# Two PSUM buffers for the scans' input in the state-space stage of a hybrid block

## The chip, the cores and the metric

The kernel is one program on one core of a Trainium2 chip. The metric is its time on the device in microseconds (us), the median of several executions; the profile comes from one more execution.

## The reference, cut to what matters

16 sequences of 256 positions and 128 features go through four residual blocks: a state-space block, a two-layer attention and feed-forward stack, a gated attention, and the same stack again. The change lies in the first, with these lines of it (width 256, 16 states):

```python
x = resid * lax.rsqrt(jnp.mean(resid * resid, -1, keepdims=True) + EPS) * norm_w
skip = x @ skip_w.T
xe = x @ in_w.T                       # then a causal convolution of 4 taps along time
xs = jax.nn.silu(xc)
delta = jax.nn.softplus(xs @ wd1.T @ wd2.T + wd2_b)
A = -jnp.exp(A_log); Bm = xs @ wb.T; Cm = xs @ wc.T
h = jnp.exp(d_l[:, :, None] * A) * h + (d_l * x_l)[:, :, None] * b_l[:, None, :]
y_l = jnp.einsum('ben,bn->be', h, c_l)
y = (y + xs * W_D) * jax.nn.silu(skip)
return resid + y @ out_w.T
```

## The kernel before, in words

**Stages.** The program runs a state-space stage ("m"), an attention and feed-forward stage ("f", 32 steps of one sequence and layer), the gated attention ("p") and "f" again. A layer norm ("n": st, mv, z on VectorE, ve, rs on GpSimd) stands in front of each.

**Tiling.** The state-space stage takes one sequence after another. Channels lie on the partitions, 256 as two halves (c), time along the free dimension. The 16 states are taken in eight groups g of two, so a tile of one group has 2 x 2 x 256 = 1024 columns. For each group:

- TensorE: bB(g) and bC(g) spread B's and C's rows over all partitions (two bf16 matmuls each, L526);
- ScalarE: a(g), four exponentials into m_a (L608), c(g), a copy of C's rows (L613);
- VectorE: bx(g), the product of delta x and B, written to PSUM (L639), and h(g), the scan over time, which reads it (L646);
- GpSimd: hc(g), the product of the states and C, as two instructions (L679);
- TensorE: y(g), the sum over states by the identity, into bank 1 (L533). y7 adds xs W_D.

Around it, once for a sequence: sq, me, rr, xr (the norm), xT and xTe (transpose and its copy), xe (convolution and projection in 16 passes, L498), xs, skip, gate, u and bc (L513), ue, hi, r1, mid, mid2, lo (B and C split in three bf16 parts), z, abs, exp, ln, delta, dx, and at the end yg, out, xx and x. xs and gate use another set of ScalarE's functions than the exponentials, so that two table loads come in each window.

**Order.** Each engine works through a list written out by hand. M_ORDER is the list of one window, in which each engine does every step once; M_STAGES says for each step how many windows it lags (0, 1 or 2), so for which sequence it is done there. The steady windows are 4 to 16. Before them stands START, a list with the first layer norms and windows 1 to 3, behind them MF with windows 17 and 18 and the first three of "f". An engine takes its list strictly in order; a step waits for semaphores of the steps that it names, and `m_before(..., g, back)` means group g - back, of this sequence or the one before.

**PSUM.** Eight banks of 512 columns: bank 0 and 1, pair 0, 1 and 2 (two banks each). In "m" before the change:

| place | holds |
|---|---|
| bank 0 | xT, u, bc |
| bank 1 | y, out |
| pair 0, first half | xe, skip, z (m_x_ps) |
| pair 0, second half | bC |
| pair 1, halves | bB, alternating by g |
| pair 2 | bx, the scans' input |

Of the kernel before, what the change touches and what calls it, by code (L numbers as in the profile page):

```python
# [64 lines left out]
class Stages:  # L65
# [13 lines left out]
    def done(self, step):  # L79
# [43 lines left out]
M_ORDER = {  # L123
    "dve": "bx1 h1 bx2 yg h2 bx3 h3 ue bx4 x h4 bx5 h5 r1 bx6 delta h6 lo bx7 h7 bx0 h0",
    "pe": "bB7 bB0 y4 bB1 bC0 y5 y6 bC1 y7 bB2 xT bC2 bB3 xe bC3 skip bB4 u bB5 out bc bC4 z bC5 y0 bB6 y1 bC6 y2 y3 "
        "bC7",
    "act": "xTe sq c2 a3 xs c3 gate a4 c4 a5 abs c5 exp hi ln a6 mid2 a7 c6 mid a0 c7 a1 c0 xr a2 c1",
    "pool": "dx hc6 xx hc7 me rr hc0 hc1 hc2 hc3 hc4 hc5"}
# [4 lines left out]
       for ph, stages in (("m", M_STAGES), ("f", F_STAGES), ("p", P_STAGES))}  # L133
# [21 lines left out]

MF = {
# [117 lines left out]
def build(nc, ins, out):  # L274
    with ExitStack() as ctx:
# [180 lines left out]
        def half(t, k):  # L456
            return t[:, 512 * k:512 * k + 512]

        m_x_ps = half(pair[0], 0).rearrange("p (c l) -> p c l", c=EC)
        m_xT_ps = bank[0][:, 0:L]  # L460
        m_u_ps = bank[0][0:DD, 0:L]
        m_bc_ps = bank[0][64:96, L:2 * L]
# [4 lines left out]
        def m_bcast(g, k):  # L467
            return (half(pair[0], 1) if k else half(pair[1], g % 2)).rearrange("p (n l) -> p n l", n=GN)
# [1113 lines left out]
```

## Time and profile before

| | |
|---|---|
| median of 3 runs | 2874.21 us (2873.69 to 2874.41) |
| the profiled execution | 2875.4 us, span 2873.6 us |
| mean granted TensorE clock | 0.977 of full speed |
| busy TensorE / VectorE / ScalarE / GpSimd | 2647.1 / 2260.1 / 2225.5 / 1223.4 us |
| the state-space stage | from the start to about 575 us |

Busy is the time in which an engine has an instruction at work. In a timeline the start is that of the instruction, and the next instruction can start a little before the one in front ends, since they overlap. "[1.16 <-ACT f_sq L872]" means that the engine was idle for 1.16 us before and that ScalarE's write of f_sq at line 872 released it. PE is TensorE, DVE VectorE, ACT ScalarE, POOL GpSimd.

### The profile page before, as it was taken

Reading aid. Unit: us, or ns where it says so; the run is one execution under the profiler, and the core shown is the slowest. Engines: PE = TensorE matmul, PEld = TensorE weight load, DVE = VectorE, ACT = ScalarE, POOL = GpSimd, SP = SyncE. Lnnn points to the kernel's source line nnn. Section 1 sums busy time; section 2 is a strip of 40 time slices with the busy share of each in tenths; the row PEclk is TensorE's granted clock in tenths of the full one; section 3 lists DMA queues with packets and bytes.
Section 4 is the critical chain, followed back from the end, with each engine's and each line's share of the span. In section 5 each row is a group of like instructions: output and inputs, shape, how many; then the busy total and the mean of one; then the engine's idle time right before and its main releaser. Section 6 shows DMA issues by size and latency. Waiting matters only on the chain. (4 is left out here: it accounts for less than half of the span.)

```text
span 2873.6 us, 55943 instructions
## 1 busy us (share of the span) xinstructions
PE 2647.1 (92%) x18868; PEld 1819.6 (63%) x18868; DVE 2260.1 (79%) x3798; ACT 2225.5 (77%) x6114; POOL 1223.4 (43%) x1089
## 2 busy tenths in 40 slices
PE   6888888789999999999999999997899999999997
PEld 3454445356666666666777777774566666666665
DVE  8999999976767777777689999996667777676774
ACT  5788878557777777777799999995677777777775
POOL 5776777664444444444400000001444444444442
PEclk8999999999999999999999999997999999999998
DMA  3000000000000000000000000000000000000000
GB/s 98 1 1 1 1 1 1 0 1 2 1 1 1 13 13 1 1 1 1 13 14 2 2 2 1 2 1 1 1 2 1 1 2 13 17 5 7 7 7 7
DMA packets 15672, 17.84 MB, mean 6 GB/s; under 512 B 3838, under 2 KB 12863, under 8 KB 15295
## 3 DMA queue, kind: packets, MB, share of 16 engines
q1 hardware_dynamic: 15390, 14.26, 1.7%
q8 instruction: 156, 2.56, 0.4%
q14 instruction: 126, 1.02, 0.1%
HBM read 12.16 MB, written 2.10 MB: 5 GB/s over the span
## 5 line engine op out<-in xcount | busy, mean ns | idle before, releaser
L1064 POOL TENSOR_TENSOR f_p<-f_p,f_rs 128x512 f32<-128x512 f32 (+1 forms) x256 | 321.2, 1255 | 907.4 <-DVE f_rs L1013 907.3
L901 ACT ACTIVATE f_p<-pair,f_nm 128x128 f32<-128x128 f32 (+1 forms) x1024 | 387.4, 392 | 125.2 <-DVE f_nm L1002 125.2
L679 POOL TENSOR_TENSOR m_hc<-m_h,m_c 128x512 f32<-128x512 f32 x256 | 323.4, 1284 | 154.5 <-DVE m_h L646 120.5
L1056 POOL TENSOR_TENSOR f_qb<-f_kn,f_tab 128x512 f32<-128x512 f32 x256 | 373.5, 1480 | 24.3 <-DVE f_kn L981 21.0
L646 DVE TENSOR_TENSOR_SCAN m_h<-m_a,pair 128x1024 f32<-128x1024 f32 x128 | 292.2, 2283 | 11.6 <-ACT m_a L608 1.9
L767 PE MATMUL pair<-f_wqkv,f_hT 128*128 128x512 f32 x512 | 248.7, 609 | 18.0 <-DVE f_kn L981 14.5
L608 ACT ACTIVATE m_a<-m_delta,m_A 128x255 f32<-128x255 f32 x512 | 217.3, 496 | 59.4 <-DVE m_h L646 58.8
L533 PE MATMUL bank<-m_hc,ident 128*128 128x512 f32 x512 | 248.2, 619 | 1.4 <-DVE X L655 1.3
L815 PE MATMUL pair<-ident,f_p 128*128 128x128 f32 x1536 | 244.7, 282 | 3.7 <-DVE f_pT L1007 2.4
L855 PE MATMUL bank<-f_hnT,f_w 128*128 128x256 f32 (+1 forms) x768 | 213.4, 401 | 12.5 <-ACT f_g L933 3.1
L815 PEld LDWEIGHTS pair<-ident,f_p 128*128 128x128 f32 x1536 | 170.6, 141 | 82.2 <-issue 60.0
L1002 DVE TENSOR_REDUCE f_nm<-pair 128x4 f32<-128x512 f32 (+1 forms) x256 | 208.3, 814 | 16.0 <-PE pair L802 13.6
L802 PE MATMUL pair<-f_kT,f_qT 64*128 64x128 f32 (+1 forms) x2048 | 211.1, 325 | 0.0
L901 ACT ACTIVATION_READ_ACCUMULATOR f_p<-pair,f_nm 128x1 f32 x1024 | 209.5, 205 | 0.0
L829 PEld LDWEIGHTS pair<-f_pT,f_v 128*64 128x64 f32 x3072 | 150.5, 137 | 91.5 <-issue 91.1
L971 DVE TENSOR_REDUCE f_ss<-f_sq 128x16 f32<-128x1024 f32 x128 | 155.5, 1215 | 64.3 <-ACT f_sq L872 64.3
L829 PE MATMUL pair<-f_pT,f_v 128*64 128x128 f32 (+1 forms) x3072 | 199.0, 265 | 2.0 <-DVE f_pT L1007 2.0
L1150 PE MATMUL pair<-p_kT,p_qT 128*128 128x256 f32 (+1 forms) x1024 | 193.1, 331 | 3.0 <-ACT p_a L1226 1.7
L1234 ACT ACTIVATE p_p<-p_s,p_rm 128x256 f32<-128x256 f32 (+1 forms) x512 | 192.0, 464 | 3.6 <-DVE p_rm L1302 3.2
L802 PEld LDWEIGHTS pair<-f_kT,f_qT 64*128 64x128 f32 x2048 | 148.5, 188 | 68.7 <-issue 68.7
L784 PE MATMUL bank<-ident,f_qa 128*128 128x128 f32 x1024 | 165.0, 284 | 14.3 <-DVE f_qa L995 8.0
L1219 ACT ACTIVATE p_e<-pair,p_hgT 128x256 f32<-128x256 f32 (+1 forms) x512 | 173.2, 429 | 4.8 <-PE bank L838 2.1
(181 smaller groups left out, 6159.2 us busy)
## 6 DMA issues: line engine op xcount, KB each, us to landing
f_wqkv<-in_f_wqkv SPq DMA_DIRECT2D x4, 768.0 KB, 4.0
out_x<-X SPq DMA_DIRECT2D x16, 128.0 KB, 1.8
f_w<-in_f_w SPq DMA_DIRECT2D x4, 341.0 KB, 3.3
f_wo<-in_f_wo SPq DMA_DIRECT2D x4, 256.0 KB, 2.7
sel<-in_sel SPq DMA_DIRECT2D x1, 768.0 KB
f_w<-in_f_w SPq DMA_DIRECT2D x4, 192.0 KB, 3.2
m_taps<-in_m_taps SPq DMA_DIRECT2D x1, 512.0 KB, 3.6
X<-in_x SPq DMA_DIRECT2D x1, 512.0 KB, 8.5
```

What stands on the lines that cost most here:

```text
L533: mm = nc.tensor.matmul(bank[1][:], ident[:], m_hc[:, g % 4, n].rearrange("p c l -> p (c l)"), start=g == 0 and n == 0, stop=False, skip_g ...
L608: op = nc.scalar.activation(m_a[:, g % 2, n, c, 1:L], m_delta[:, b, c, 1:L], ACT.Exp, scale=m_A[:, c, g * GN + n:g * GN + n + 1])
L646: op = nc.vector.tensor_tensor_scan(m_h[:, g % 2].rearrange(flat), m_a[:, g % 2].rearrange(flat), pair[2][:], 0.0, ALU.mult, ALU.add)
L679: op = nc.gpsimd.tensor_tensor(m_hc[:, g % 4, n], m_h[:, g % 2, n], m_c[:, g % 2, n].unsqueeze(1).broadcast_to([P, EC, L]), ALU.mult)
L767: mm = nc.tensor.matmul(half(pair[0], x), f_hT[:, t * P:t * P + P], fw["wqkv"][:, x * 512:x * 512 + 512], start=True, stop=True)
L802: mm = nc.tensor.matmul(SC[:, slot(h), k0:k1], f_qT[r, b, h // 2, t * P:t * P + P], f_kT[r, b, h // 2, k0:k1], start=False, stop=True, ski ...
L815: mm = nc.tensor.transpose(PT_PS[:, j * P:j * P + P], f_p[:, t, j, y * P:y * P + P], ident[:])
L829: mm = nc.tensor.matmul(OT_F[DH * e:DH * e + DH, c, q0:q1], f_v[:, b, y, h, :], w, start=y == 1 or t == 0, stop=y == 0, skip_group_check=True)
L855: mm = nc.tensor.matmul(bank[1][0:HR[c], e * L:e * L + L], fw["w1"][:, x * HID + c * P:x * HID + c * P + HR[c]], f_hnT[:], start=True, sto ...
L901: op = nc.scalar.activation(f_p[:, t, j, k0:k1], SC[:, j, k0:k1], ACT.Exp, bias=f_nm[:, t, j:j + 1], accum_out=f_sm[:, t, j:j + 1])
L1056: op = nc.gpsimd.tensor_tensor(f_qb[:, t, :, o].rearrange("p (x h) d -> p x h d", x=2), f_kn[:, t, :, 32 - 32 * e:64 - 32 * e].rearrange(" ...
L1064: op = nc.gpsimd.tensor_tensor(f_p[:, t, :, k0:k1], f_p[:, t, :, k0:k1], f_rs[:, t, :].unsqueeze(2).broadcast_to([P, 4, k1 - k0]), ALU.mult)
```

## The change

The scans' input gets two buffers, pair 1 and pair 2 by turns. For that B's broadcast gets one bank (pair 0, first half) where it had two, C's keeps one, and xe, skip and z move into bank 0 to xT, u and bc. The waits follow: bx(g) waits for h(g-2) where it waited for h(g-1); bB(g) for bx(g-1) where it was bx(g-2); xT for delta of the sequence before where it was lo; u and bc for gate where it was xs; z for r1 besides ue; the first qk0 of "f" for bx7 besides c7. The lists of the window, of START and of MF are written anew, with other lags for some steps.

```diff
 M_STAGES = [
-    "sq me rr xr xT xe skip u bc ue z r1 delta lo bx0 h0",
-    "bB0 bC0 y0 bB1 bC1 bx1 h1 y1 bB2 bC2 bx2 h2 y2 bB3 bC3 bx3 h3 y3 bB4 bC4 bx4 h4 bB5 bC5 bB6 bC6 mid xx "
-    "xTe xs gate hi abs exp ln mid2 dx bC7 a0 c0 a1 c1 a2 bx5 h5 bx6 h6 bx7 h7 hc0 hc1 hc2 hc3 hc4 hc5",
-    "yg out x y6 y7 y4 y5 a3 a4 c2 c3 a5 c4 a6 c5 c6 a7 c7 hc6 hc7 bB7"]
+    "sq me rr xr xT xe skip u bc ue z r1 delta lo bx0 h0 xTe bx1 h1 bx2",
+    "bB0 bC0 y0 bB1 bC1 y1 bB2 bC2 h2 bB3 bC3 bx3 h3 bB4 bC4 bx4 h4 bB5 bC5 bB6 bC6 mid xs gate hi abs exp ln "
+    "mid2 dx a0 c0 a1 c1 bx5 h5 bx6 h6 bx7 h7 hc0 yg",
+    "out x y6 y7 y4 y5 a3 a4 c2 c3 a5 c4 a6 c5 c6 a7 c7 hc6 hc7 bB7 y2 y3 bC7 a2 xx hc1 hc2 hc3 hc4 hc5"]
 M_ORDER = {
-    "dve": "bx1 h1 bx2 yg h2 bx3 h3 ue bx4 x h4 bx5 h5 r1 bx6 delta h6 lo bx7 h7 bx0 h0",
-    "pe": "bB7 bB0 y4 bB1 bC0 y5 y6 bC1 y7 bB2 xT bC2 bB3 xe bC3 skip bB4 u bB5 out bc bC4 z bC5 y0 bB6 y1 bC6 y2 y3 "
-        "bC7",
-    "act": "xTe sq c2 a3 xs c3 gate a4 c4 a5 abs c5 exp hi ln a6 mid2 a7 c6 mid a0 c7 a1 c0 xr a2 c1",
-    "pool": "dx hc6 xx hc7 me rr hc0 hc1 hc2 hc3 hc4 hc5"}
+    "dve": "h2 bx3 x h3 bx4 ue h4 bx5 r1 h5 bx6 delta bx7 h6 lo h7 bx0 h0 bx1 h1 bx2 yg",
+    "pe": "y2 bB7 y3 bC7 y4 bC0 bB0 y5 y6 xT bB1 bC1 y7 bC2 bB2 xe bC3 out bB3 skip bB4 bC4 bc u y0 bB5 bC5 y1 bC6 z "
+        "bB6",
+    "act": "a2 c2 sq a3 xs c3 gate a4 c4 hi a5 c5 a6 abs exp ln c6 a7 mid2 mid c7 a0 xr a1 c0 xTe c1",
+    "pool": "me hc1 hc2 hc3 xx hc4 rr hc5 dx hc6 hc7 hc0"}
...
 START = {
-    "dve": "n1: st mv z n2: st c0: nw inc n3: st n4: st n2: mv n3: mv n2: z n4: mv n5: st n6: st n7: st n8: st n5: "
-        "mv n6: mv n7: mv n9: st n8: mv n3: z c0: skip A n4: z n5: z n10: st n9: mv c0: ones n11: st n12: st m1: ue "
+    "dve": "n1: st mv z n2: st n3: st c0: nw inc skip n2: mv n3: mv n4: st n2: z c0: A n3: z n5: st n6: st n7: st "
+        "n4: mv n5: mv c0: ones n6: mv n7: mv n8: st mv m1: ue r1 n9: st n10: st n9: mv n11: st n12: st n13: st n10: "
+        "mv n11: mv n12: mv n13: mv n4: z n14: st m1: delta lo n5: z n15: st n16: st m1: bx0 n14: mv m1: h0 bx1 n15: "
...
-    "act": "m1: sq xr m2: xTe sq c0: exp m2: xs gate abs exp hi ln mid2 mid a0 a1 c0 xr a2 c1 m3: xTe sq c2 a3 xs c3 "
+    "act": "m1: sq xr xTe c0: exp m2: sq xs gate hi abs exp ln mid2 mid a0 xr a1 c0 xTe c1 m3: a2 c2 sq a3 xs c3 gate "
...
-    "pool": "c0: small n1: ve rs m1: me rr n2: ve rs n3: ve c0: wide_p n4: ve n5: ve n3: rs n4: rs n5: rs n6: ve n7: "
+    "pool": "c0: wide_p small wide_f n1: ve rs m1: me rr n2: ve n3: ve n2: rs n3: rs m2: me n4: ve n5: ve n6: ve n7: "
...
 MF = {
-        "h4 bx5 n3: mv m17: h5 n5: st n4: mv n5: mv m17: bx6 f1: hT m17: h6 n6: st m17: bx7 f1: ss0 cl0 n7: st n8: "
-        "st f1: kn0 m17: h7 f1: qa0 ss1 cl1 qs0 kn1 qa1 n9: st n10: st n6: mv m18: yg n7: mv f1: qs1 n11: st m18: x "
+        "h5 n4: mv m17: bx6 f1: hT m17: bx7 n5: mv m17: h6 h7 f1: ss0 cl0 n6: st n7: st f1: kn0 n8: st n9: st n6: mv "
+        "f1: qa0 ss1 cl1 qs0 kn1 n7: mv f1: qa1 m17: yg n10: st n11: st f1: qs1 m18: x n8: mv n9: mv n10: mv n11: mv "
...
-        m_x_ps = half(pair[0], 0).rearrange("p (c l) -> p c l", c=EC)
+        m_x_ps = bank[0][:].rearrange("p (c l) -> p c l", c=EC)
...
-        m_bx_ps = pair[2][:].rearrange("p (n c l) -> p n c l", n=GN, c=EC)
+        def m_bx_ps(g):
+            return pair[1 + g % 2][:].rearrange("p (n c l) -> p n c l", n=GN, c=EC)
 
         def m_bcast(g, k):
-            return (half(pair[0], 1) if k else half(pair[1], g % 2)).rearrange("p (n l) -> p n l", n=GN)
+            return half(pair[0], k).rearrange("p (n l) -> p n l", n=GN)
...
                 pe.wait_ge(*act_m.at(i, "xr"))
-                pe.wait_ge(*dve_m.at(i - 1, "lo"))
+                pe.wait_ge(*dve_m.at(i - 1, "delta"))
...
             elif s == "xe":
...
-                pe.wait_ge(*dve_m.at(i - 1, "delta"))
...
             elif s == "u" or s == "bc":
...
-                pe.wait_ge(*act_m.at(i, "xs"))
+                pe.wait_ge(*act_m.at(i, "gate"))
...
                 pe.wait_ge(*dve_m.at(i, "ue"))
-                pe.wait_ge(*act_m.at(i, "gate"))
+                pe.wait_ge(*dve_m.at(i, "r1"))
...
-                pe.wait_ge(*(m_before(dve_m, i, "bx", g, 2) if k == "bB" else m_before(act_m, i, "c", g, 1)))
+                pe.wait_ge(*(m_before(dve_m, i, "bx", g, 1) if k == "bB" else m_before(act_m, i, "c", g, 1)))
...
                 dve.wait_ge(*pe_m.at(i, f"bB{g}"))
-                dve.wait_ge(*m_before(dve_m, i, "h", g, 1))
-                op = nc.vector.tensor_tensor(m_bx_ps, m_dx[:, b].unsqueeze(1).broadcast_to([P, GN, EC, L]),
+                dve.wait_ge(*m_before(dve_m, i, "h", g, 2))
+                op = nc.vector.tensor_tensor(m_bx_ps(g), m_dx[:, b].unsqueeze(1).broadcast_to([P, GN, EC, L]),
...
-                                                  pair[2][:], 0.0, ALU.mult, ALU.add)
+                                                  pair[1 + g % 2][:], 0.0, ALU.mult, ALU.add)
...
                 if t == 0 and i == 1:
                     pe.wait_ge(*act_m.at(NSEQ, f"c{M_LAST}"))
+                    pe.wait_ge(*dve_m.at(NSEQ, f"bx{M_LAST}"))
```

## Rows read from the trace of the kernel before

**Rows 1.** The page, TensorE of part 1 and the scan of part 5.

```profile
PE 2647.1 (92%) x18868; PEld 1819.6 (63%) x18868; DVE 2260.1 (79%) x3798; ACT 2225.5 (77%) x6114; POOL 1223.4 (43%) x1089
...
L646 DVE TENSOR_TENSOR_SCAN m_h<-m_a,pair 128x1024 f32<-128x1024 f32 x128 | 292.2, 2283 | 11.6 <-ACT m_a L608 1.9
```

**Rows 2.** The page, part 2: VectorE's busy tenths in 40 slices.

```profile
DVE  8999999976767777777689999996667777676774
```

**Rows 3.** Windows: stretch, length, busy PE, PEld, DVE, ACT, POOL, PEclk, DMA.

```profile
297.00:329.00 32.00, 27.86 (x106) 14.90 (x105) 30.52 (x23) 25.83 (x58) 22.91 (x21) 0.97 0.00 1
...
521.00:553.00 32.00, 22.37 (x75) 10.78 (x72) 31.42 (x41) 16.35 (x37) 19.75 (x19) 0.79 0.00 1
...
35.00:521.00 486.00, 423.08 (x1622) 231.48 (x1621) 463.28 (x351) 385.28 (x860) 344.55 (x308) 0.97 0.00 1
```

**Rows 4.** Timeline of VectorE, one window: start us, length us, what.

```profile
291.46 2.28 DVE L646 TENSOR_TENSOR_SCAN m_h<-m_a,pair 128x1024 f32<-128x1024 f32 x1
...
294.21 1.23 DVE L639 TENSOR_TENSOR pair<-m_dx,pair 128x1024 f32<-128x1024 f32 x1
295.58 2.29 DVE L646 TENSOR_TENSOR_SCAN m_h<-m_a,pair 128x1024 f32<-128x1024 f32 x1
298.00 1.23 DVE L639 TENSOR_TENSOR pair<-m_dx,pair 128x1024 f32<-128x1024 f32 x1
...
305.56 1.23 DVE L639 TENSOR_TENSOR pair<-m_dx,pair 128x1024 f32<-128x1024 f32 x1
306.70 0.68 DVE L651 TENSOR_TENSOR m_yg<-bank,m_gate 128x512 f32<-128x512 f32 x1
307.30 2.28 DVE L646 TENSOR_TENSOR_SCAN m_h<-m_a,pair 128x1024 f32<-128x1024 f32 x1
...
323.46 2.28 DVE L646 TENSOR_TENSOR_SCAN m_h<-m_a,pair 128x1024 f32<-128x1024 f32 x1
```

**Rows 5.** Timeline of VectorE, start and second join.

```profile
89.19 0.57 DVE L704 TENSOR_SCALAR Z<-X,lmv,lrs 128x128 f32<-128x128 f32 x2
...
101.99 1.61 DVE L704 TENSOR_SCALAR Z<-X,lmv,lrs 128x128 f32<-128x128 f32 x2
...
524.45 2.29 DVE L646 TENSOR_TENSOR_SCAN m_h<-m_a,pair 128x1024 f32<-128x1024 f32 x1
526.65 1.23 DVE L694 BATCH_NORM_STATS2 lst<-X 128x6 f32<-128x128 f32 x6
```

**Rows 6.** Timeline of TensorE, a window and the second join.

```profile
304.90 3.62 PE L498 MATMUL pair<-m_xT,m_inc 128*128 128x256 f32 x16
...
317.52 1.88 PE L533 MATMUL bank<-m_hc,ident 128*128 128x512 f32 x4
319.24 0.38 PE L526 MATMUL pair<-m_bc,sel 96*128 96x256 bf16 x2
...
532.94 0.59 PE L526 MATMUL pair<-m_bc,sel 96*128 96x256 bf16 x2 [2.19 <-DVE pair L639]
```

**Rows 7.** Timeline of ScalarE, one window.

```profile
303.75 0.57 ACT L613 ACTIVATE m_c<-pair 128x512 f32<-128x512 f32 x1
...
305.64 1.70 ACT L608 ACTIVATE m_a<-m_delta,m_A 128x255 f32<-128x255 f32 x4
...
312.73 1.71 ACT L608 ACTIVATE m_a<-m_delta,m_A 128x255 f32<-128x255 f32 x4
```

**Rows 8.** Timeline of GpSimd, one window.

```profile
301.82 2.50 POOL L679 TENSOR_TENSOR m_hc<-m_h,m_c 128x512 f32<-128x512 f32 x2 [0.36 <-DVE m_h L646]
```

**Rows 9.** Timelines of GpSimd, ScalarE and VectorE, the start.

```profile
25.12 1.80 POOL L1459 MEMSET f_p<- 128x2048 f32 x1
...
15.35 0.23 ACT L1398 ACTIVATE m_A<-m_A_log 128x32 f32<-128x32 f32 x1 [1.08 <-DMA sel<-in_sel]
...
34.23 2.29 DVE L646 TENSOR_TENSOR_SCAN m_h<-m_a,pair 128x1024 f32<-128x1024 f32 x1
```

**Rows 10.** Timeline of VectorE, second join.

```profile
556.00 1.22 DVE L971 TENSOR_REDUCE f_ss<-f_sq 128x16 f32<-128x1024 f32 x1 [1.16 <-ACT f_sq L872]
```

54 rows, old and new, of tables (MF, START) are left out of this document.

## The prediction

> **What bounds the kernel now.** I read the page first: over the whole span TensorE is the busy engine, VectorE second [rows 1]. The slices say where that is false: in slices 2 to 8 VectorE is at 90% or more [rows 2], the state-space stage, about a fifth of the span. The changed steps lie only there and in its two joins; the stages behind it have the same code. So the question is what VectorE's stretch is worth.
>
> The windows view puts numbers to it: in one window of 32 us VectorE is busy 30.52, TensorE 27.86, ScalarE 25.83, GpSimd 22.91; from 35 to 521 us the mean granted TensorE clock is 0.97 [rows 3]. The timeline gives the window's length: the scan h6 of one sequence starts at 291.46, of the next at 323.46, so a sequence costs 32.00 us [rows 4], and 1.5 us of it are gaps in VectorE. No other engine makes it wait: over the 128 scans the idle time ended by ScalarE is 1.9 us in all [rows 1]. What fills the gaps is the order inside VectorE. The reader is to compare start with next start in rows 4:
>
> - a scan right behind its own product (294.21 to 295.58): 1.37 us; something independent behind a product (305.56 to 306.70): 1.14. Difference 0.23.
> - a product right behind the scan before it (295.58 to 298.00): 2.42; something independent behind a scan (524.45 to 526.65 [rows 5]): 2.20. Difference 0.22.
>
> The product must wait for that scan only because both use the one buffer, pair 2. Five of the eight products and five of the eight scans of a window stand so. Check of the reading: 5 x 2.42 + 3 x 2.20 + 5 x 1.37 + 3 x 1.14, with 2.7 for the six small steps (yg takes 0.60 from start to start [rows 4]) and 0.3 for small gaps at r1, lo and delta, is 31.9 against 32.00 measured.
>
> **The change part by part.**
>
> *Two scan buffers, and the list of VectorE.* No product waits for the scan in front of it any more, it needs the one two back. In the new list seven scans have a product behind them (2.20 each), one has lo (2.31): 17.7. Two products (bx0, bx1) still have their own scan right behind: 2 x 1.37 = 2.7. bx7 has h6 behind it, whose product is older, and x, ue, yg, delta stand behind four others: 5 x 1.14 = 5.7; r1 behind bx5 takes 1.3. With 2.7 for the small steps the window is 30.15 us. I take 30.2: 1.8 us less than 32.00. Nothing is added on VectorE: the same 8 products, 8 scans and 6 small steps.
>
> *One bank for B's broadcast.* bB(g) now waits for bx(g-1), one back where it was two. From product to next product this is a round trip VectorE, TensorE, VectorE. Row 532.94 shows the first half: TensorE starts 0.14 us after the product ends (531.57 + 1.23), and two matmuls take 0.59 at a low clock there, or 0.38 at a high one (319.24) [rows 6]. With about 0.05 back it is 0.55 to 0.8. Behind seven of the products at least one scan of 2.20 passes before the next product, which hides it. The place without one is bx6, delta, bx7: bx7 could start 0.6 us after bx6's end, so it costs 0 to 0.2, if TensorE's queue is empty then. TensorE takes its list in order: in front of bB7 is y2, 1.72 us (317.52 to 319.24 [rows 6]), in front of that bB6 and z, and z now waits for r1. From r1's end z 1.0, bB6 0.25, y2 1.72 make 3.0; from r1's end to bx6's end VectorE takes 2.2 + 1.2 + 0.03 = 3.4. So TensorE is free 0.4 us before it is needed. If it were not, bx7, h6 and all behind would move by what is missing.
>
> *Projections in one bank.* xT, xe, skip, bc, u and z share bank 0 now, so each waits until the one before is read out: xT for delta, bc and u for gate, z for r1. Behind z stand bB6, y2 and bB7, behind xT stand bB1, bC1 and y7, behind bc and u stand y0 and bB5. delta closes the sequence z, abs, exp, ln: from r1's end 0.1 + 1.0 + 0.6 + 0.65 + 0.75 = 3.1 (estimates from ScalarE's 128x512 rows such as 303.75, 0.57 [rows 7], with some overhead), against 0.03 + 2.2 + 1.14 = 3.4 on VectorE. It fits by 0.3.
>
> The tightest ring goes through ScalarE. From h0's end: hc0 0.17 + 2.50 [rows 8], c2 and the two squares 1.2 (by the c at 303.75), then from a3's start to a4's start 7.09 (305.64 to 312.73: a3, a table load, xs, its skip matmul, gate, another table load), a4 1.71 [rows 7], 0.1 to VectorE: 12.8. VectorE's own way from h0's end to h4 is -0.1 + 1.37 + 2.20 + 1.14 + 0.60 + 2.20 + 1.14 + 0.33 + 2.20 + 1.14 + 0.31 = 12.5. So a4 is late by about 0.2 to 0.3 us in each window. Bounds: nothing, if the chain overlaps better (gate stands closer to xs when skip finds TensorE free); 0.9, if xs is also late: xe, 3.5 us (304.90 [rows 6]), now starts only behind y7, which waits for hc7. I take 0.2 a window: 1.6 us saved of the 1.8. Thirteen windows (4 to 16) give 13 x 1.6 = 20.8.
>
> *First join.* GpSimd's wide fills go ahead of the first layer norm's steps; the longest takes 1.80 us [rows 9], together I take some 2 to 4 us on that way. VectorE's skip step moves before mv and z of sequence 2, and waits there for the last weights, which are there at 15.3 (ScalarE's exp of A at 15.35 is released by them [rows 9]). With that z2, sq of sequence 2, and behind it on ScalarE a table load and xs of sequence 1 come about 3 us later than before. Before, though, z's matmul of sequence 1 waited for VectorE, which was busy with layer-norm steps; now three fewer z steps stand there. By my count from step to step delta of sequence 1 ends near 30.8, and h0 starts at 34.2 as before (34.23 [rows 9]): 0, bounds -1 to +3. The three z steps come back behind h0. A z takes 0.57 or 1.61 depending on what GpSimd does meanwhile [rows 5]: 3 x 1.3 = 3.9 us, bounds 1.7 to 4.8. And windows 2 and 3 gain less, since z and mv steps stood in about half of their gaps already: +1.7 (2 x 1.6 less 1.5). Sum of the start: 2.2 us lost, bounds 6 lost to 1 gained.
>
> The Trainium skill bears on those z steps. Rows 5 show the same operation at 0.57 and 1.61. "SBUF — State Buffer", section "Who interferes with whom", says that such a VectorE instruction and GpSimd exclude each other on a shared port pair for a whole instruction. At an unhindered 0.57 the sum would lose 1.7 there and not 3.9, by the rule's full blocking nearer 3.9; the trace agrees with the rule.
>
> *Second join.* qk0 of the next stage takes over pair 0 and so waits for bx7 too, not for c7 alone; c7 needs hc5 and stays the later one. h7 comes before the first sum of squares and no longer behind kn0, so that y7, yg and x have their input earlier. The steps of VectorE are the same, and it idled little there (1.16 us at 556.00 [rows 10]); TensorE was at 22.37 of 32 us with the clock at 0.79 [rows 3]. I take a gain of 1, bounds 3 lost and 3 gained. Behind the join TensorE sets the pace with the same list, so that the shift stays to the end.
>
> **Sum.** 20.8 - 2.2 + 1.0 = 19.6 us. The profiled execution took 2875.4 with a span of 2873.6; its span becomes 2854.0. The median of the runs shown is 2874.2, 1.2 below the profiled one: 2874.2 - 19.6 = 2854.6.
>
> **The rivals.**
>
> 1. *Full gain.* Nothing is late in the windows: 13 x 1.8 = 23.4, the start costs nothing, the join gives 3: 2848. For it: TensorE needs 27.9 of 30.2 us. Against: the ScalarE sum above. 0.15.
>
> 2. *A ring takes half.* ScalarE's chain through xs and gate, or TensorE's from hc7 over y7, xe, out to bB3, sets a window of 31.1: 13 x 0.9 = 11.7, less 2.2, plus 1: 2863.7. For it: two margins of 0.3 to 0.4 us and one below zero, sums of durations without any slack for handing over. 0.22.
>
> 3. *No gain.* The gaps belong to every pair of VectorE instructions and not to the dependence. Then the windows stay at 32.0 and the start loses 2.2: 2875. Against it: 1.14 beside 1.37 and 2.20 beside 2.42 in the same trace; the only thing that differs is who reads what was just written. 0.06. The Trainium skill speaks for it: "VectorE: DVE Perf Modes", section "The DRAIN you can't avoid", says that the pipe empties behind each operation and that a semaphore between two of them costs nothing extra. By that rule the sum is 0 in the windows, by rows 4 and 5 it is 1.8 in each; the trace disagrees with the rule.
>
> 4. *Slower: the single bank of B.* The in-order list of TensorE puts a y (1.72 us) or xe (3.5) between a product's end and the next bB when the bB comes up too late. One such miss at bx7 and one at bx3 (bB3 stands behind xe, bC3 and out, by my count ready 0.1 us before bx3) cost up to 3.4 us a window: 13 x (3.4 - 1.8) = 21 more, plus 1.2: 2896. It decides as soon as misses pass 1.8 us a window; at 2 it would be 2.6 + 1.2 slower, 2878. Speaks for it that TensorE would be busy 92% of the window; against, that both places have some margin and a late VectorE lets TensorE catch up. 0.07.
>
> The forecast case has 0.5.
>
> **How the numbers follow.** About 0.2% (5.7 us) is what a measurement of this kernel tells from no change, so faster means below 2868.5. Forecast case and rivals 1 and 2 lie there, 0.87, less 0.03 for the far end of rival 2: 0.84. Same: rival 3 with that tail, 0.09. Slower: rival 4 and a bad start of the pipeline together, 0.07. The range has rival 1's end with all gains at once, 2846, and rival 2 with a bad start and join, 2868; outside are rivals 3 and 4 and the tails, about 0.18.
>
> **What would show it.** Scans of one step should start 30.2 to 30.6 us apart where they were 32.00. In VectorE's timeline a product should start 2.20 behind a scan everywhere, and only h0 and h1 should stand 1.37 behind their product. A gap before h4 released by m_a is the ScalarE ring; one before bx7 or bx3 released by TensorE is rival 4's place. h0 of sequence 1 should start near 34. The prediction is wrong if products still start 2.42 behind scans, if the windows' length is set by TensorE waits, or if the next stage does not begin some 20 us earlier.

## The result, and the profile after

The changed kernel took 2856.88 us (median of 5 runs, 2849.61 to 2863.93), the kernel before beside it 2874.28 (5 runs, 2873.69 to 2874.43): ratio 0.994, 95% interval 0.9923 to 0.9956. That is 17.4 us less; 19.6 were forecast. The profiled execution took 2858.1 us with a span of 2856.3, 17.3 less than before in both. The page of the changed kernel, the lines that answer to [rows 1, 2]:

```profile
PE 2650.9 (93%) x18868; PEld 1813.7 (63%) x18868; DVE 2253.8 (79%) x3798; ACT 2236.6 (78%) x6114; POOL 1220.2 (43%) x1089
...
DVE  7999999886677677777689999996767776776774
...
L646 DVE TENSOR_TENSOR_SCAN m_h<-m_a,pair 128x1024 f32<-128x1024 f32 x128 | 292.0, 2282 | 4.4
```

The busy times are nearly the same (VectorE 2260.1 and 2253.8 us, its scans 292.2 and 292.0): nothing became faster, idle time went. Before the scans it fell from 11.6 us [rows 1] to 4.4, and no releaser is named any more. The windows view of the changed kernel, columns as in [rows 3]:

```profile
35.00:503.00 468.00, 425.81 (x1631) 227.48 (x1632) 461.60 (x358) 395.12 (x864) 346.21 (x308) 0.98 0.00 1
297.00:327.20 30.20, 28.28 (x112) 15.16 (x111) 29.78 (x23) 26.41 (x59) 22.89 (x20) 1.00 0.00 1
...
610.40:613.00 2.60, 2.60 (x22) 2.15 (x22) 2.60 (x6) 0.72 (x3) 1.16 (x1) 0.50 0.02 6
614.50:618.30 3.80, 3.80 (x38) 2.94 (x36) 3.80 (x7) 1.35 (x3) 3.64 (x6) 1.00 0.00 0
620.00:624.00 4.00, 4.00 (x14) 1.66 (x16) 1.43 (x3) 2.10 (x9) 1.04 (x1) 0.57 0.00 0
```

In a window VectorE is now busy 29.78 of 30.20 us, 0.42 idle where it was 1.48 [rows 3]. VectorE's timeline of the changed kernel, in several places:

```profile
25.50 0.42 DVE L621 COPY m_u<-bank 64x256 f32<-64x256 f32 x1 [5.73 <-PE bank L513]
...
30.64 0.69 DVE L633 SCALAR_TENSOR_TENSOR m_delta<-bank,m_t 128x512 f32<-128x512 f32 x1 [0.66 <-ACT m_t L600]
...
35.64 2.29 DVE L646 TENSOR_TENSOR_SCAN m_h<-m_a,pair 128x1024 f32<-128x1024 f32 x1
...
109.21 2.28 DVE L646 TENSOR_TENSOR_SCAN m_h<-m_a,pair 128x1024 f32<-128x1024 f32 x1
...
288.14 2.29 DVE L646 TENSOR_TENSOR_SCAN m_h<-m_a,pair 128x1024 f32<-128x1024 f32 x1
290.35 1.21 DVE L639 TENSOR_TENSOR pair<-m_dx,pair 128x1024 f32<-128x1024 f32 x1
291.69 2.29 DVE L646 TENSOR_TENSOR_SCAN m_h<-m_a,pair 128x1024 f32<-128x1024 f32 x1
...
308.72 1.21 DVE L639 TENSOR_TENSOR pair<-m_dx,pair 128x1024 f32<-128x1024 f32 x1
309.96 0.42 DVE L625 TENSOR_TENSOR m_r<-bank,m_bc 32x256 f32<-32x256 f32 x1
310.42 2.29 DVE L646 TENSOR_TENSOR_SCAN m_h<-m_a,pair 128x1024 f32<-128x1024 f32 x1
312.62 1.21 DVE L639 TENSOR_TENSOR pair<-m_dx,pair 128x1024 f32<-128x1024 f32 x1
313.73 0.68 DVE L633 SCALAR_TENSOR_TENSOR m_delta<-bank,m_t 128x512 f32<-128x512 f32 x1
314.44 1.23 DVE L639 TENSOR_TENSOR pair<-m_dx,pair 128x1024 f32<-128x1024 f32 x1
...
321.88 2.29 DVE L646 TENSOR_TENSOR_SCAN m_h<-m_a,pair 128x1024 f32<-128x1024 f32 x1
...
502.99 2.29 DVE L646 TENSOR_TENSOR_SCAN m_h<-m_a,pair 128x1024 f32<-128x1024 f32 x1
...
611.69 6.33 DVE L704 TENSOR_SCALAR Z<-X,lmv,lrs 128x128 f32<-128x128 f32 x8
...
619.08 0.41 DVE L967 COPY f_hT<-bank 64x256 f32<-64x256 f32 x1
...
646.62 0.42 DVE L967 COPY f_hT<-bank 64x256 f32<-64x256 f32 x1 [0.26 <-PE bank L757]
```

The reader is to see: h0 of one sequence starts at 291.69, of the next at 321.88, 30.19 us apart where h6 was 32.00 apart [rows 4]. A product stands 2.20 to 2.21 behind a scan (288.14 to 290.35), no longer 2.42. h0 still stands 1.34 behind its own product.

To follow the gain along the time, the same instructions of the kernel before are needed. The first scan is in [rows 9], h0 of sequence 16 in [rows 5]; here are h0 of sequence 3, two runs of z and the copy f_hT of steps 4 and 5 of "f", in VectorE's timeline of the kernel before:

```profile
105.17 2.27 DVE L646 TENSOR_TENSOR_SCAN m_h<-m_a,pair 128x1024 f32<-128x1024 f32 x1
...
626.89 1.65 DVE L704 TENSOR_SCALAR Z<-X,lmv,lrs 128x128 f32<-128x128 f32 x2
...
631.45 5.87 DVE L704 TENSOR_SCALAR Z<-X,lmv,lrs 128x128 f32<-128x128 f32 x10
...
637.57 0.41 DVE L966 COPY f_hT<-bank 64x256 f32<-64x256 f32 x1
...
663.49 0.42 DVE L966 COPY f_hT<-bank 64x256 f32<-64x256 f32 x1 [0.27 <-PE bank L757]
```

| | before | after | shift | gained in between |
|---|---|---|---|---|
| first scan | 34.23 | 35.64 | +1.41 | -1.4 |
| h0 of sequence 3 | 105.17 | 109.21 | +4.04 | -2.6 |
| h0 of sequence 16 | 524.45 | 502.99 | -21.46 | +25.5 |
| f_hT of step 4 | 637.57 | 619.08 | -18.49 | -3.0 |
| f_hT of step 5 | 663.49 | 646.62 | -16.87 | -1.6 |
| end | | | -17.3 | +0.4 |

The last column is what the kernel gained since the row above. So the windows gave 25.5 us, and both joins, the start and the passage into "f", took 8.6 of them back. Where the second join loses, TensorE's timeline of the changed kernel shows:

```profile
313.97 0.38 PE L526 MATMUL pair<-m_bc,sel 96*128 96x256 bf16 x2 [0.40 <-DVE pair L639]
...
609.21 1.17 PE L856 MATMUL bank<-f_hnT,f_w 128*128 128x256 f32 x4 [2.58 <-DVE f_u L1040]
...
619.98 3.39 PE L768 MATMUL pair<-f_wqkv,f_hT 128*128 128x512 f32 x4 [1.62 <-DVE f_hT L968]
```

It idled 2.58 us for u1 (L1040), in front of which two z steps stand in VectorE's list (1.55 and 1.00 us), and 1.62 for f_hT, behind the long run of z. Behind each of the two the granted clock fell: it was 0.50 from 610.4 to 613.0, 1.00 again from 614.5 to 618.3, and 0.57 from 620 to 624, where the matmuls qk0 took 3.39 us. At the same places in the kernel before, one z stood ahead of u1 (626.89), and TensorE waited 0.93 there and 1.82 at f_hT, behind which qk0 took 1.99:

```profile
628.98 1.13 PE L855 MATMUL bank<-f_hnT,f_w 128*128 128x256 f32 x4 [0.93 <-DVE f_u L1039]
...
638.47 1.99 PE L767 MATMUL pair<-f_wqkv,f_hT 128*128 128x512 f32 x4 [1.82 <-DVE f_hT L967]
```

### The profile page after: what moved, and what is told of

It reads as the page before. It is cut to its first block and busy times, and to the rows that moved or that the text cites. A ratio compares the mean times of both kernels' runs of the same rounds, so it can differ in the third digit from the quotient of the medians.

```text
span 2856.3 us, 55927 instructions
## 1 busy us (share of the span) xinstructions
PE 2650.9 (93%) x18868; PEld 1813.7 (63%) x18868; DVE 2253.8 (79%) x3798; ACT 2236.6 (78%) x6114; POOL 1220.2 (43%) x1089
## 5 line engine op out<-in xcount | busy, mean ns | idle before, releaser
L646 DVE TENSOR_TENSOR_SCAN m_h<-m_a,pair 128x1024 f32<-128x1024 f32 x128 | 292.0, 2282 | 4.4
```

The source lines that it names most:

```text
L646: op = nc.vector.tensor_tensor_scan(m_h[:, g % 2].rearrange(flat), m_a[:, g % 2].rearrange(flat), pair[1 + g % 2][:], 0.0, ALU.mult, ALU.add)
```

## The experiments

The kernel before, measured beside each group of runs, had medians of 2873.7 to 2875.4 us, so a difference of about 1 us between two of the kernels below says nothing. What the second join lost or gained is counted from here on as the shift of f_hT of step 5 less that of h0 of sequence 16, against the kernel before: 4.6 us lost in the changed kernel.

### one_buffer: everything but the second buffer

```diff
-    "dve": "h2 bx3 x h3 bx4 ue h4 bx5 r1 h5 bx6 delta bx7 h6 lo h7 bx0 h0 bx1 h1 bx2 yg",
+    "dve": "h2 bx3 x h3 bx4 ue h4 bx5 r1 h5 bx6 delta h6 bx7 lo h7 bx0 h0 bx1 h1 bx2 yg",
...
-            return pair[1 + g % 2][:].rearrange("p (n c l) -> p n c l", n=GN, c=EC)
+            return pair[2][:].rearrange("p (n c l) -> p n c l", n=GN, c=EC)
...
-                dve.wait_ge(*m_before(dve_m, i, "h", g, 2))
+                dve.wait_ge(*m_before(dve_m, i, "h", g, 1))
```

The swap of bx7 and h6 also stands in START and MF; one buffer can't do without it.

> The changed kernel with one scan buffer again: both products and scans use pair 2, a product waits for the scan right before it, and the list has h6 ahead of bx7 (with one buffer the other order cannot run). All else, B's single bank, the projections in bank 0, the ScalarE, TensorE and GpSimd lists, stays as changed. Theory A (a product that waits for the scan in front starts 0.22 us later): all eight products stand behind a scan, so the window grows from 30.20 to about 31.9 us and the whole from 2857 to about 2882, above the kernel before. Theory B (the gap behind an instruction does not depend on who reads its output; the gain came from the other lists, which removed ScalarE's stalls): the window stays at 30.2 to 30.5 us and the time at 2857.

Measured: 2884.81 us (4 runs, 2882.1 to 2885.22), ratio 1.0036 (1.0023 to 1.005). VectorE's timeline of this kernel:

```profile
305.62 2.29 DVE L648 TENSOR_TENSOR_SCAN m_h<-m_a,pair 128x1024 f32<-128x1024 f32 x1
308.04 1.23 DVE L641 TENSOR_TENSOR pair<-m_dx,pair 128x1024 f32<-128x1024 f32 x1
...
337.49 2.29 DVE L648 TENSOR_TENSOR_SCAN m_h<-m_a,pair 128x1024 f32<-128x1024 f32 x1
```

The product is back at 2.42 behind its scan, the window is 31.87 us. Against the 32.00 of before all the other edits give 0.13 us, the buffer the other 1.7: eight products 0.22 later each, less the 0.11 that bx7 loses behind delta in the changed kernel. That the kernel is slower than before comes from its ends: h0 of sequence 3 starts at 113.11 (7.9 late), h0 of sequence 16 at 528.77 (4.3 late), f_hT of step 5 at 671.86 (8.4 late).

### direct_scans: both buffers, each scan right behind its own product

```diff
-    "dve": "h2 bx3 x h3 bx4 ue h4 bx5 r1 h5 bx6 delta bx7 h6 lo h7 bx0 h0 bx1 h1 bx2 yg",
+    "dve": "h2 bx3 h3 x bx4 h4 ue bx5 h5 r1 bx6 h6 delta bx7 lo h7 bx0 h0 bx1 h1 yg bx2",
```

START and MF are those of one_buffer.

> The changed kernel with both buffers, but VectorE's list of the window puts each scan right behind its own product (seven of eight instead of two): h2 bx3 h3 x bx4 h4 ue bx5 h5 r1 bx6 h6 delta bx7 lo h7 bx0 h0 bx1 h1 yg bx2. Theory A: five more pairs at 1.37 instead of 1.14 us, so the window goes from 30.20 to about 31.3 us and the whole to about 2872. Theory B: the window stays at 30.2 us. If the window grows by more than 1.3 us, some wait of another engine has come in, which a gap before the instruction would name.

Measured: 2907.57 us (4 runs, 2906.8 to 2908.12), ratio 1.0118 (1.0104 to 1.0131). VectorE's timeline:

```profile
287.52 2.29 DVE L648 TENSOR_TENSOR_SCAN m_h<-m_a,pair 128x1024 f32<-128x1024 f32 x1
...
301.39 0.42 DVE L627 TENSOR_TENSOR m_r<-bank,m_bc 32x256 f32<-32x256 f32 x1
304.53 1.23 DVE L641 TENSOR_TENSOR pair<-m_dx,pair 128x1024 f32<-128x1024 f32 x1 [2.71 <-issue]
...
321.64 2.29 DVE L648 TENSOR_TENSOR_SCAN m_h<-m_a,pair 128x1024 f32<-128x1024 f32 x1
```

and TensorE's in the same place:

```profile
301.96 2.04 PE L522 MATMUL bank<-m_u,m_wd 65*128 65x256 f32 x4 [3.46 <-DVE m_r L627]
303.80 0.63 PE L528 MATMUL pair<-m_bc,sel 96*128 96x256 bf16 x2
```

The window is 34.12 us (287.52 to 321.64). Five more scans stand 1.36 behind their product, each 0.23 more: about 1.2 of the 3.9 over 30.2. The rest is a wait of 2.71 that no theory had; the profile names no releaser for it, but bx6 starts 0.10 behind the end of bB6 (303.80 + 0.63). r1 now comes right ahead of bx6, z waits for r1, bB6 stands behind z in TensorE's list, and bx6 needs bB6. TensorE had idled 3.46 us before z, and z took 2.04 instead of some 1.1. So this run doesn't price the pairs alone, and its forecast of about 2872 us was missed. What it shows is a relative of rival 4: the same strict list on TensorE, but the step that blocks it is z, which waits for r1 because the projections share bank 0, and not a y or xe in front of a late bB. One small step in the wrong place costs more than all that the second buffer gives.

### join_z: two z steps of the second join moved

```diff
-        "n15: mv f3: hT nm00 pe111 n8: z n16: mv f3: rs00 n9: z f3: ss0 cl0 nm10 kn0 z1 qa0 rs10 st mv nm01 ss1 hn "
-        "cl1 qs0 rs01 kn1 n10: z f3: qa1 n11: z f3: nm11 u1 pe101 qs1 u0 rs11 n12: z n13: z n14: z n15: z f3: z2 "
+        "n15: mv f3: hT nm00 pe111 n8: z n16: mv f3: rs00 n9: z f3: ss0 cl0 nm10 kn0 z1 qa0 rs10 n10: z f3: st mv "
+        "nm01 ss1 hn cl1 qs0 rs01 kn1 qa1 nm11 u1 pe101 qs1 u0 rs11 n11: z n12: z n13: z n14: z n15: z f3: z2 "
```

> The changed kernel with two layer-norm steps of the second join moved: z of sequence 10 goes from between kn1 and qa1 of the third attention step to the place behind rs10, where VectorE idled 1.7 us, and z of sequence 11 from before nm11 to behind rs11. Theory C (these two steps, 1.55 and 1.00 us, pushed u1 back, TensorE then idled 2.58 us and its granted clock fell, which cost the rest of the 4.8 us lost between the third and the fifth f_hT): most of the 4.8 comes back, the time falls by 3 to 5 us to about 2853. Rival D (the loss is the usual cost of filling the pipeline there and comes from the earlier start itself): no change beyond 1 us.

Measured: 2857.97 us (5 runs, 2857.86 to 2858.54), ratio 0.9946 (0.9933 to 0.9958): no gain. TensorE's timeline of this kernel:

```profile
617.52 3.78 PE L769 MATMUL pair<-f_wqkv,f_hT 128*128 128x512 f32 x4 [3.69 <-DVE f_hT L969]
```

The long wait at u1 is gone, but the run of z behind it has grown to ten instructions (6.32 us), TensorE waits 3.69 for f_hT, and qk0 then takes 3.78. f_hT of step 5 starts 18.2 earlier than before, against 16.9, but 0.55 of that was there at h0 of sequence 16 already (502.44): the join loses 3.8 us where it lost 4.6. Most of what was saved at u1 was lost again some microseconds on, and the 3 to 5 us that were expected did not come.

### again: the changed kernel once more

Nothing is edited. The five runs of the changed kernel lay 14 us apart, those of the kernel before 0.7; join_z's only 0.7.

> The changed kernel unchanged, for another profile: its five executions spread from 2849.6 to 2863.9 us where the kernel before stays within 0.8. Theory E (the joins between stages, where TensorE's load is patchy, are executed at a granted clock of 1.2 or 2.4 GHz by chance of the moment, and the steady windows are always alike): the windows of the state-space stage measure 30.20 again, and the difference to the first profile lies in the joins with another granted clock there. Rival F: the state-space windows themselves vary, since their margins are small: some profile shows windows of 30.5 us or more.

Measured: 2856.98 us (5 runs, 2854.65 to 2860.59), ratio 0.9941 (0.9928 to 0.9955). The windows are 30.20 again. The first scan starts at 36.82, and VectorE once waits for the projection behind a matmul that ran at the lower clock (VectorE's timeline, then TensorE's):

```profile
128.05 0.42 DVE L621 COPY m_u<-bank 64x256 f32<-64x256 f32 x1 [2.01 <-PE bank L513]
```

```profile
119.14 1.16 PE L545 MATMUL bank<-m_out_w,m_yg 128*128 128x128 f32 x8 [1.39 <-DVE m_yg L651]
...
121.38 2.08 PE L505 MATMUL bank<-m_xT,m_skip_w 128*128 128x256 f32 x4 [0.86 <-ACT m_xs L577]
```

From 121.38 to 123.46 the granted clock was 0.50. The first of the windows took 33.58 us by it, where it was 31.48 in the first profile. The last weights landed at 14.61, 0.8 later than in the first profile (13.82); whether that made the first scan late is not shown, since in join_z, with the same START and weights at 13.84, it starts at 35.01. The second join lost 6.2 us here. So the steady windows repeat to 0.02 us, and what differs between runs comes in at the start, in the first windows, at the second join and behind it.

### start_back: START's head as before

```diff
-    "dve": "n1: st mv z n2: st n3: st c0: nw inc skip n2: mv n3: mv n4: st n2: z c0: A n3: z ...
+    "dve": "n1: st mv z n2: st mv c0: nw inc n3: st mv n2: z n4: st c0: skip A n3: z ...
-    "act": "m1: sq xr xTe c0: exp m2: sq xs ...
+    "act": "m1: sq xr xTe m2: sq c0: exp m2: xs ...
-    "pool": "c0: wide_p small wide_f n1: ve rs m1: me rr n2: ve n3: ve n2: rs n3: rs m2: me ...
+    "pool": "c0: small n1: ve rs m1: me rr n2: ve rs n3: ve rs c0: wide_p wide_f m2: me ...
```

> The changed kernel with the head of START nearly as before: GpSimd's wide fills stand behind the first three layer norms' steps instead of ahead of them, VectorE's skip step, which waits for the last weights, comes after z of sequence 2 instead of before, and ScalarE does sq of sequence 2 before the exponential of A. Theory G (these moves made the first scan late: 35.0, 35.6 and 36.8 us in three profiles of the changed START, later the later the last weights landed, 13.8 to 14.6, where it was 34.23 before with weights at about 15.2): the first scan starts at 32 to 33 us, the time falls by 2 to 4 us to about 2853 to 2855. Rival H (the start is bound by the landing of the last weights whatever the order): the first scan stays at 35 us or more and the time at 2857.

Measured: 2852.23 us (5 runs, 2851.18 to 2853.58), ratio 0.9923 (0.991 to 0.9935), 4.7 less than the changed kernel. VectorE's timeline:

```profile
21.85 0.42 DVE L622 COPY m_u<-bank 64x256 f32<-64x256 f32 x1 [2.79 <-PE bank L514]
...
31.02 2.29 DVE L647 TENSOR_TENSOR_SCAN m_h<-m_a,pair 128x1024 f32<-128x1024 f32 x1
```

The wait for the first ue is 2.79 us instead of 5.73 and the first scan comes 4.6 us earlier. The new head of START (GpSimd's fills and VectorE's skip ahead of sequence 2's norm), whose sum with the freer VectorE behind it the prediction put at nothing, costs that much. The three lists were put back together, so which of the moves counts is not separated.

### join_z2: three z steps in gaps of the second join

z8 goes ahead of the third f_hT, z10 behind rs10, z11 behind nm11, so that the run behind u stays at eight instructions.

```diff
-        "n15: mv f3: hT nm00 pe111 n8: z n16: mv f3: rs00 n9: z f3: ss0 cl0 nm10 kn0 z1 qa0 rs10 st mv nm01 ss1 hn "
-        "cl1 qs0 rs01 kn1 n10: z f3: qa1 n11: z f3: nm11 u1 pe101 qs1 u0 rs11 n12: z n13: z n14: z n15: z f3: z2 "
+        "n15: mv n8: z f3: hT nm00 pe111 n16: mv f3: rs00 n9: z f3: ss0 cl0 nm10 kn0 z1 qa0 rs10 n10: z f3: st mv "
+        "nm01 ss1 hn cl1 qs0 rs01 kn1 qa1 nm11 n11: z f3: u1 pe101 qs1 u0 rs11 n12: z n13: z n14: z n15: z f3: z2 "
```

> The changed kernel with the layer-norm steps z of the second join spread: z8 ahead of the third f_hT, where VectorE idled 2.9 us, z10 behind rs10, z11 behind nm11, so that before the fourth f_hT five z are left in a row as in the kernel before, and not six as in the first trial (join_z), which took away the wait at u1 and got a longer one at f_hT. Theory C2 (the loss of 4.8 us between the third and the fifth f_hT is the run of z steps, each slow beside GpSimd, and the fall of the granted clock behind a TensorE wait of over 2.5 us): TensorE's wait at the fourth f_hT is near 1.8 to 2.8 us, and 3 to 4 of the 4.8 us come back, time about 2853 to 2854. Rival D: no change beyond 1 us, with the loss at some other wait.

Measured: 2854.06 us (5 runs, 2853.02 to 2855.44), ratio 0.9928 (0.9916 to 0.9941), 2.8 less than the changed kernel. f_hT of step 5 starts 18.6 earlier than before, h0 of sequence 16 21.9 (502.55): the join loses 3.3 us, 1.3 less than in the changed kernel. In the profiled executions 2.3 us more came in behind f_hT of step 5, where the code is the same. As start_back, with the join as in the changed kernel, loses 4.0, these 1.3 us are little more than the spread. TensorE's timeline shows that the place itself is not healed, 2.67 us idle and qk0 slow:

```profile
617.00 3.78 PE L769 MATMUL pair<-f_wqkv,f_hT 128*128 128x512 f32 x4 [2.67 <-DVE f_hT L969]
```

### long_bB7: bB7's two matmuls done three times

It writes the same values three times, which lengthens the trip from bx6 over bB7 to bx7.

```diff
-                    for n in range(GN):
+                    for n in list(range(GN)) * (3 if s == "bB7" else 1):
```

> The changed kernel with the two matmuls of B's broadcast for group 7 done three times over (same output), so that the round trip from bx6's end to bx7 over the single bank takes about 0.43 us longer. Theory I (this trip has no margin: bx7 starts 0.71 us behind delta where the step alone would take 0.60): the window grows by 0.35 to 0.45 us to 30.6, the whole by 5 to 7 us, and nothing else changes. Rival J (the 0.11 us is not a wait, there is slack of the size that the sum of rows gave, 0.1 to 0.2 us, or TensorE's late queue adds more): window +0.2 or less, or well over 0.5.

Measured: 2864.93 us (5 runs, 2857.99 to 2868.43), ratio 0.9964 (0.9952 to 0.9976). VectorE's timeline:

```profile
314.82 2.29 DVE L646 TENSOR_TENSOR_SCAN m_h<-m_a,pair 128x1024 f32<-128x1024 f32 x1
...
318.13 0.68 DVE L633 SCALAR_TENSOR_TENSOR m_delta<-bank,m_t 128x512 f32<-128x512 f32 x1
319.28 1.23 DVE L639 TENSOR_TENSOR pair<-m_dx,pair 128x1024 f32<-128x1024 f32 x1 [0.47 <-issue]
...
345.45 2.29 DVE L646 TENSOR_TENSOR_SCAN m_h<-m_a,pair 128x1024 f32<-128x1024 f32 x1
```

The window is 30.63, 0.43 longer for 0.44 us more of matmuls: in the changed kernel this trip has no margin. It costs the 0.11 us by which bx7 starts behind delta's 0.60 (313.73 to 314.44). Thirteen windows make 5.6 us; the medians differ by 8.0, and five runs that lie 10 us apart don't say where the rest is.

This kernel has the join of the changed one, with the same wait of 2.58 at u1, and yet the join loses 1.1 us only. TensorE's timeline shows the difference, a wait of 1.18 at f_hT and qk0 at full speed:

```profile
625.57 1.98 PE L768 MATMUL pair<-f_wqkv,f_hT 128*128 128x512 f32 x4 [1.18 <-DVE f_hT L968]
```

### best: the two repairs together, and two more moves

START's head as in start_back, the second join as in join_z2, z4 to z6 ahead of the first ue, and bx7 behind h6.

```diff
-    "dve": "h2 bx3 x h3 bx4 ue h4 bx5 r1 h5 bx6 delta bx7 h6 lo h7 bx0 h0 bx1 h1 bx2 yg",
+    "dve": "h2 bx3 x h3 bx4 ue h4 bx5 r1 h5 bx6 delta h6 bx7 lo h7 bx0 h0 bx1 h1 bx2 yg",
```

> The changed kernel with the head of START and the second join as in start_back and join_z2, three z steps of START (4 to 6) moved ahead of the first ue, where VectorE idled about 6 us, and bx7 behind h6 in the window's list (bx6 delta h6 bx7 lo h7), which takes the single-bank trip off the path. Expected if theories G and C2 hold: windows of 30.1 us (1.3 us less in 13), 3 to 4 us from the start, 3 from the z steps, 3 to 4 from the join, in all about 2846 to 2848 us. If both rivals hold: 2856.

Measured: 2850.24 us (5 runs, 2848.49 to 2852.37), ratio 0.9915 (0.9901 to 0.9928). The swap gave nothing: the window is 30.21, and from h5 to h7 it is 7.94 us where it was 7.92. The trace shows both sides: behind delta h6 now starts after 0.60 and not 0.71, but lo takes 0.56 us behind bx7 where it took 0.41 behind h6. Why lo is longer there was not tried. The first scan started at 31.86, with the last weights at 16.14, and at 121 us ue waited 2.04 as in the run "again". The three z steps, expected to give 3 us, took 1.9 from the way between the first scan and h0 of sequence 3 (71.36 us, 73.24 in start_back). Together the edits give 6.6 us, where the two repairs one by one gave 4.7 and 2.8; the forecast was 2846 to 2848.

### xb_late: what makes z slow

join_z2, and GpSimd's adds xb of sequences 10 to 16 wait until the last z is done.

```diff
-                pool.wait_ge(ln_z, i)
+                pool.wait_ge(ln_z, i + (6 if i == NSEQ + 10 else 0))
```

> join_z2 with one more edit: GpSimd's adds of the last bias to X for sequences 10 to 16 of the second join wait until z of sequence 16 is done, so that they no longer run beside the row of z steps on VectorE. Theory K (the eight z instructions in front of the fourth f_hT take 5.8 us only because GpSimd's adds and they exclude each other; alone one pair takes 0.57, and TensorE's wait of 2.7 us behind them is what brings its granted clock down, which costs another 2.8 us in the step behind): the eight take 2.2 to 2.8 us, TensorE's wait at the fourth f_hT falls under 1 us, the qk0 matmuls behind it take 1.9 instead of 3.8 us, and the time falls by 3 to 6 us from 2854 to about 2849. Rival L (the z steps are slow by themselves, or the clock falls anyway): less than 1 us.

Measured: 2851.27 us (4 runs, 2850.66 to 2855.53), ratio 0.9921 (0.9906 to 0.9936). VectorE's timeline of this kernel at the run of eight z:

```profile
609.93 3.69 DVE L705 TENSOR_SCALAR Z<-X,lmv,lrs 128x128 f32<-128x128 f32 x8
```

the same run in join_z2:

```profile
609.21 5.83 DVE L705 TENSOR_SCALAR Z<-X,lmv,lrs 128x128 f32<-128x128 f32 x8
```

and TensorE's timeline of xb_late behind it:

```profile
615.28 1.98 PE L769 MATMUL pair<-f_wqkv,f_hT 128*128 128x512 f32 x4 [0.23 <-DVE f_hT L969]
```

The same eight instructions take 2.1 us less without the adds beside them, TensorE waits 0.23 and not 2.67, and qk0 is back at 1.98. f_hT of step 5 starts 22.65 us earlier than before, h0 of sequence 16 20.95 (503.50): the join gains 1.7 us where it lost 3.3 in join_z2 and 4.6 in the changed kernel. So 5.0 us come from the adds alone: this is the loss of the second join, shown. Of the forecast the two sizes were off: the eight z were to take 2.2 to 2.8 us, and the median fell by 2.8 where 3 to 6 were expected, since this execution gained less behind the join.

### best2: xb_late with START's head as before

The edits of start_back and of xb_late together.

> xb_late together with start_back's head of START: 4 to 5 us from the start on top, 2844 to 2847 us, and the lowest of all kernels here. If theory K falls: about 2849 to 2850.

Measured: 2845.59 us (4 runs, 2844.72 to 2848.19), ratio 0.9897 (0.9881 to 0.9914), the fastest here, 5.7 below xb_late beside it on the same chip. f_hT of step 5 starts at 637.09, 26.4 earlier than before; the join gains 1.2 us again. Work on the joins alone, without touching a window, gave 11.3 us more than the change had.

## Why the prediction was right, point by point

**What bounds the stage, and the gain: right in kind.** VectorE's own order set the window. A product no longer waits for the scan ahead of it, 2.20 instead of 2.42, and six products instead of three have an independent instruction behind them, 1.13 later (1.24 for r1), where their own scan came after 1.37. one_buffer takes the buffer away and the gain with it. Rival 3 is out. The Trainium skill ("VectorE: DVE Perf Modes", section "The DRAIN you can't avoid") says that a semaphore between two VectorE instructions costs nothing extra; where the wait is for the instruction right in front the runs disagree, 31.87 against 30.20 us for the same 22 instructions of a window.

**The size of the windows' term: 25.5, not 20.8.** Two parts. The kernel before took 32.25 us a window on the average (105.17 to 524.45, 13 windows): some windows had waits for m_a, 1.9 us in all [rows 1], and the first, with a z in it, was 1.3 longer. The forecast took the 32.00 of one window for all: 3.3 us. The new windows took 30.29 on the average (109.21 to 502.99, again with a z in the first) where 30.4 stood: 1.4 us. The 0.2 that ScalarE's ring was to cost did not come; no scan of the steady windows waits for m_a. Rival 2 is out, rival 1 right about the windows.

**B's single bank: 0.1 in a window, as priced.** TensorE starts bB7 0.14 behind bx6's end (312.62 + 1.21 to 313.97), as row 532.94 had shown [rows 6], and had idled 0.40 us before, the 0.4 that the prediction counted. bx7 is 0.11 late; the bounds were 0 to 0.2. Rival 4 didn't come. Its own case, a y or xe in front of a late bB, was not run; direct_scans shows what one blocked step in TensorE's list costs, and long_bB7 that the trip at bx7 has no margin.

**Start: 4.0 lost, not 2.2.** The z steps behind the first scan were priced nearly right: from the first scan to h0 of sequence 3 the kernel lost 2.6 where the forecast had 3.9 - 1.7 = 2.2. What failed is the step "delta of sequence 1 ends near 30.8, and h0 starts at 34.2 as before": the first scan came 1.4 later, and with the old head it comes 3.2 earlier than before (31.02). In the changed kernel delta ended at 31.33, 0.5 late, and the first scan stood 4.3 us behind it, where the forecast left 3.4. The prediction names no lower clock there; in the trace skip, bc and u took 1.65, 1.88 and 1.97 us on TensorE, behind idle times of 2.58 and 0.78, where they had taken 1.10, 1.05 and 1.08 in the kernel before, behind an idle time of 2.74. How much of the 1.4 that makes was not tried. It all lay within the bounds that were given.

**Second join: the step that failed.** "The steps of VectorE are the same, and it idled little there ... I take a gain of 1, bounds 3 lost and 3 gained." It lost 4.6. The steps are the same, but two z steps stand ahead of u1 where one did, and TensorE waited 2.58 there, not 0.93; then ten instructions of z stand in front of f_hT in both kernels, and from the first of them to f_hT it took 7.39 us (611.69 to 619.08) and not 6.12 (631.45 to 637.57); and behind that qk0 took 1.4 us longer than before, at the lower clock. join_z2 and xb_late show it: with z steps in gaps 1.3 us are back, with the adds out of the way 6.3 in all, and the join then gains 1.7, near the 1 that was forecast. The prediction had the price of a disturbed z, 1.61 against 0.57 [rows 5], and used it at the start only; it put no price on a fall of the clock. One part is chance: with the same join the loss was 4.6, 6.2 (again) and 4.0 (start_back) us, and 1.1 in long_bB7, where the clock was at its full level for qk0.

**The sum.** 25.5 - 4.0 - 4.6 + 0.4 = 17.3, forecast 20.8 - 2.2 + 1.0 = 19.6. The total is near partly by luck: one miss of +4.7 and two of -1.8 and -5.6 cancel in part. The gain of the windows was there in full and more; the joins gave a third of it back.

## What to carry to other kernels

When an engine's own in-order stream is the bound, compare start to next start of neighbouring instructions, dependent and independent; a second buffer that lets them be crossed is worth the difference times their number, and it can be counted before building. Then price the two ends of the pipeline as carefully as the steady part: here the joins cost a third of what the windows gave, and work on them brought another 11.3 us, where the change had brought 17.4. Small VectorE steps like z belong beside a quiet GpSimd, and not right ahead of the step that TensorE waits for.

## What the runs showed of the hardware

- **A short idle of TensorE can be paid twice.** qk0 took 1.98 us behind an idle of 0.23 (xb_late), 1.18 (long_bB7) and 1.23 (one_buffer), and 1.99 behind 1.82 (before), but 3.78 behind 2.67 (join_z2), 2.72 (start_back) and 3.69 (join_z), 2.42 behind 3.17 (again), and 3.39 behind 1.62 (after). The granted clock was 0.57 in the last of these, so most of the stretch ran at the lower of its two levels, 1.2 GHz. The length of the idle doesn't decide alone: 1.62 was followed by a fall and 1.82 not; and of the waits of 2.58 at u1 those in the changed kernel and in long_bB7 were (0.50 from 610.4 to 613.0 and from 617 to 619), the one in start_back was not (1.00 from 602.9 to 610). In the run "again" idle times of 1.39 and 0.86 stood in front of a skip of 2.08 us; in the first profile they were 0.78 and 0.86, and skip took 1.13.
- **Where the spread comes from.** The changed kernel's runs lie 14 us apart, 5.9 in the second measurement; those of the kernel before 0.7, and 3.9 beside the later runs. The steady windows repeat to 0.02 us; with the same START the first scan came at 35.0 (join_z) to 36.8 (again), one window had a wait of 2 us or not, and behind f_hT of step 5, where all the kernels have the same code, they gained up to 2.7 us on the kernel before (best, again) or lost 2.0 (long_bB7). What makes the clock fall at one of these places in one run and not in the next stays open.
- **Two small steps don't overlap with their neighbours.** r1 starts 0.03 us behind the end of bx5 (308.72 + 1.21 to 309.96) and h5 0.04 behind its end, while most other pairs overlap by 0.08. The Trainium skill has a rule for it ("VectorE: DVE Perf Modes", section "Two Vector instructions with no wait between them"): an instruction whose input or output starts in another quarter of the partitions than the last one read or written in the same memory is held until all earlier ones end. The trace agrees: r1 reads and writes the slice of partitions from 64, lo reads there, their neighbours start at 0, and each side costs some 0.1 us.
- **Eight z took 6.33 and 5.83 us** with the adds of GpSimd beside them, and 3.69 with the adds behind them. Four times the 0.57 of an undisturbed pair [rows 5] is 2.3; GpSimd still had two other instructions, 1.48 and 0.72 us, beside those of xb_late. The rule of the shared port pair in the Trainium skill ("SBUF — State Buffer", section "Who interferes with whom"), named in the prediction, fits.
